# A vision-transformer tower on one core: a ring of twelve exponentials, softmax sums turned in blocks on DVE, and V in two buffers

## What is computed

```python
qkv = fake_quant(x, sx1, zx1) @ fake_quant(ww1, sw1, zw1).T
q, k, v = jnp.split(qkv, 3, axis=-1)
dots = jnp.einsum('bhnd,bhmd->bhnm', fake_quant(q, sq, zq), fake_quant(k, sk, zk)) * scale
a = jax.nn.softmax(dots, axis=-1)
out = jnp.einsum('bhnm,bhmd->bhnd', fake_quant(a, sa, za), fake_quant(v, sv, zv))
return fake_quant(out, sx2, zx2) @ fake_quant(ww2, sw2, zw2).T + bb2
```

## Time and profile before

| what | value |
|---|---|
| median of 3 runs | 1808.92 us (1805.69 to 1816.67) |
| the profiled execution | 1809.49 us, its span 1807.5 us |
| busy: PE, DVE, ACT, POOL | 1448.1 (80%), 1430.0 (79%), 1023.6 (57%), 420.5 us (23%) |
| mean granted TensorE clock | 0.765 |
| chain that ended last | PE 51%, issue 19%, DVE 18%, ACT 7% |
| products pi, 384 | 380.7 us busy on DVE |
| reciprocals of the sums, 192 | 267.7 us busy on DVE |
| exponentials, 384 | 316.2 us busy on ACT, 255.1 us idle ahead of them |

### The profile page before, as it was taken

The page is one execution under the profiler, slowest core; times in us unless marked ns, Lnnn a source line. Parts: engine busy times, 40 slices in busy tenths (PEclk is TensorE's granted clock), DMA queues, the critical chain, the costliest instruction groups (busy, mean ns, idle before and its releaser), DMA issues.

```text
span 1807.5 us, 41731 instructions
## 1 busy us (share of the span) xinstructions
PE 1448.1 (80%) x11806; PEld 846.6 (47%) x11806; DVE 1430.0 (79%) x2863; ACT 1023.6 (57%) x2005; POOL 420.5 (23%) x540
## 2 busy tenths in 40 slices
PE   5999858888887878987898888888798476666765
PEld 5999824444444444444444444444444233333332
DVE  4557827878778787788878888777878789999997
ACT  0000035666666565566656666555656378888887
POOL 6444400000000000000000000000000166666664
PEclk9999956768769686589758787666957567778778
DMA  7899712222223232233223232222323222223232
GB/s 238 272 278 299 223 48 76 89 89 86 81 89 96 85 96 84 80 97 92 85 79 94 83 97 86 85 85 86 90 78 90 83 62 83 83 78 87 83 87 65
DMA packets 154934, 192.00 MB, mean 106 GB/s; under 512 B 40208, under 2 KB 117072, under 8 KB 154576
## 3 DMA queue, kind: packets, MB, share of 16 engines
q1 hardware_dynamic: 99120, 154.10, 28.4%
q10 hardware_dynamic: 55776, 37.45, 7.0%
HBM read 156.99 MB, written 34.50 MB: 106 GB/s over the span
## 4 chain that ended last, share of the span: by engine, by line
PE 51%; issue 19%; DVE 18%; ACT 7%; ACTq 2%; DMA 2%; DVEq 1%; POOL 0%; SPq 0%
PE psum L1054 10%; PE psum L1170 10%; PE psum L1110 8%; DVE pi L923 7%; PE psum L1158 5%; PE psum L1117 5%; PE psum L1127 4%; PE psum L1192 3%; PE psum L1129 2%; DVE qkb L787 2%; DVE xring L1012 2%; ACT qki L519 2%; ACT wraw L557 1%; DVE yb L1037 1%; ACT att L533 1%
## 5 line engine op out<-in xcount | busy, mean ns | idle before, releaser
L557 ACT ACTIVATE wraw<-psum 128x788 f32<-128x788 f32 (+1 forms) x384 | 316.2, 824 | 255.1 <-DVE pi L923 249.2
L902 DVE RECIPROCAL weff<-psum 128x197 f32<-128x197 f32 x192 | 267.7, 1394 | 213.8 <-PE psum L1170 213.8
L923 DVE TENSOR_TENSOR pi<-wraw,weff 128x788 int16<-128x788 f32 (+1 forms) x384 | 380.7, 991 | 0.3 <-DMA weff<-z_row 0.3
L701 POOL TENSOR_TENSOR h<-hin,att 128x192 f32<-128x192 f32 (+1 forms) x128 | 83.8, 655 | 1122.2 <-ACT att L533 1122.2
L1170 PE MATMUL psum<-wraw,sa_cols 128*32 128x197 f32 (+1 forms) x3072 | 270.2, 433 | 15.6 <-DVE weff L902 15.2
L1110 PE MATMUL psum<-xT,w1b 96*128 96x197 bf16 x1536 | 239.8, 310 | 43.2 <-ACT xT L515 43.2
L519 ACT ACTIVATE qki<-psum 128x394 int16<-128x394 f32 x384 | 178.3, 494 | 89.1 <-PE psum L1110 88.3
L1110 PEld LDWEIGHTS psum<-xT,w1b 96*128 96x128 bf16 x1536 | 154.2, 118 | 148.9 <-issue 91.0
L1054 PE MATMUL psum<-weff,xring 128*128 128x192 f32 (+1 forms) x1168 | 196.7, 331 | 19.5 <-DVE weff L746 16.8
L787 DVE TENSOR_SCALAR pT<-pi,lo,hi 128x788 bf16<-128x788 int16 (+1 forms) x384 | 190.7, 497 | 24.9
L1054 PEld LDWEIGHTS psum<-weff,xring 128*128 128x128 f32 (+1 forms) x1168 | 192.8, 192 | 20.5 <-DVE weff L746 16.8
(11 more groups left out here) (108 smaller groups left out, 2017.1 us busy)
## 6 DMA issues: line engine op xcount, KB each, us to landing
weff<-z_row SPq DMA_DIRECT2D x192, 394.0 KB, 3.4
xring<-xt SPq DMA_DIRECT2D x98, 384.0 KB, 4.3
tin<-h_att SPq DMA_DIRECT2D x49, 192.0 KB, 2.5
tres<-h_att ACTq DMA_DIRECT2D x49, 192.0 KB, 2.6
out<-oo ACTq DMA_DIRECT2D x49, 192.0 KB, 2.6
h_res<-hp ACTq DMA_DIRECT2D x96, 96.0 KB, 3.8
hin<-h_res SPq DMA_DIRECT2D x64, 96.0 KB
h_att<-h SPq DMA_DIRECT2D x64, 96.0 KB
```

The source lines that it names most:

```text
L557: act.activation(ex[0:r, u, :, :].rearrange("p (a h) n -> p a h n", a=2), psum[0:r, 2 * (u % 2):2 * (u % 2) + 2, 0:2 * N] .rearrange("p a ...
L902: v.reciprocal(zinv[:, g, :], psum[:, 4, 0:N]).then_inc(s_zinv, 1)
L923: v.tensor_tensor(pi[0:r, t, :, 0:N], ex[0:r, w % U1, :, :], zb[0:r, g, :, :], ALU.mult).then_inc(s_pi, 1)
```

## The change

The arrays `wraw`, `weff`, `wmix` and `xring` become parts of one array `big`, so that `ex` can take twelve units instead of six. ACT's exponential now waits for the product twelve units back. The lags on DVE grow by two slots: TT_LAG 5 to 7, CLIP_LAG 6 to 8, and the pieces `o` of SLOTS move accordingly. V has two buffers ahead of its clip, and the clip moves from slot 1 to slot 5. The reciprocal of 128x197 becomes three operations: a turn of the sums out of PSUM in blocks of 32x32 (224 = 7 x 32 columns, the last 27 padded with ones), after which the 32 equal rows of a head are 32 equal columns; a reciprocal of one column of each of the seven blocks; a turn back into `zinv`. PE may overwrite the sums once they are turned.

```diff
-        wraw = sb("wraw", [128, KC, 5, D], fp32)
-        weff = sb("weff", [128, 4, KC, D], fp32)
-        wmix = sb("wmix", [128, 2, 2, D], fp32)
-        xring = sb("xring", [128, PACK, KC * 128], fp32)
+        NR, NF, ND = KC * 5 * D, 4 * KC * D, 4 * D
+        big = sb("big", [128, NR + NF + ND + PACK * KC * 128], fp32)
...
-        ex = stage[:, 0:24 * N].rearrange("p (u h n) -> p u h n", u=6, h=4)
+        NEX, NZ = 48 * N, 224
+        ex = big[:, 0:NEX].rearrange("p (u h n) -> p u h n", u=12, h=4)
+        zb = big[:, NEX:NEX + 12 * N].rearrange("p (g h n) -> p g h n", g=3, h=4)
+        zt = sb("zt", [128, NZ // 32, 32], fp32)
+        zti = sb("zti", [128, NZ // 32, 32], fp32)
+        zinv = sb("zinv", [128, 3, NZ], fp32)
...
-        SLOTS = [[("v", 3, 0), ("o", 2, -2), ("xt", 0, 1)],
+        SLOTS = [[("v", 3, 0), ("o", 1, -2), ("xt", 0, 1)],
                  [("qk", 0, 1), ("qk", 1, 1), ("v", 0, 1)],
-                 [("o", 0, -1), ("qk", 2, 1)],
+                 [("o", 2, -2), ("qk", 2, 1)],
                  [("qk", 3, 1), ("qk", 4, 1), ("qk", 5, 1)],
-                 [("o", 1, -1), ("y", 0, -2)],
+                 [("o", 0, -1), ("y", 0, -2)],
                  [("y", 1, -2), ("v", 1, 1), ("v", 2, 1)]]
...
-        TT_LAG, CLIP_LAG = 5, 6
+        TT_LAG, CLIP_LAG = 7, 8
...
-                        wait(act, s_vb, im)
+                        wait(act, s_vb, im - 1)
...
-                        wait(act, s_pi, U - 5)
+                        wait(act, s_pi, U - 11)
...
+                    summed = u % 2 == 0 and has_unit(b, u - 2)
+                    if summed:
+                        dve.wait_ge(s_zsum, G + 1)
+                        wait(dve, s_zti, G)
+                        v.transpose(zt[:, :, :].rearrange("p a b -> p (a b)"), psum[:, 4, 0:NZ]).then_inc(s_zt, 1)
                     if has_unit(b, u - CLIP_LAG):
...
-                    if u % 2 == 0 and has_unit(b, u - 2):
-                        G, g = 3 * b + u // 2 - 1, (u // 2 - 1) % 3
-                        dve.wait_ge(s_zsum, G + 1)
-                        v.reciprocal(zinv[:, g, :], psum[:, 4, 0:N]).then_inc(s_zinv, 1)
-                    if u == 1 and exists(b, 0):
+                    if summed:
+                        dve.wait_ge(s_zt, G + 1)
+                        wait(dve, s_zinv, G)
+                        v.reciprocal(zti[:, :, 0], zt[:, :, 0]).then_inc(s_zti, 1)
+                    if u == 5 and exists(b, 0):
...
+                    if summed:
+                        dve.wait_ge(s_zti, G + 1)
+                        wait(dve, s_zrow[g], 16 * (b - 1 if u == 0 else b))
+                        v.transpose(zinv[:, g, :], zti[:, :, :].rearrange("p a b -> p (a b)")).then_inc(s_zinv, 1)
...
-                            wait(pe, s_zinv, G)
+                            wait(pe, s_zt, G)
```

More of the change, by code:

```diff
@@ L90, in vit_tower_kernel @@
         xb = sb("xb", [128, 2, PACK, D], bf16)
-        stage = wraw[:, :, :, :].rearrange("p a b c -> p (a b c)")
+        stage = big[:, 0:NR]
         stage_i = sb("stage_i", [128, 2 * 3 * INNER], i16)
@@ L158, in vit_tower_kernel @@
         s_zsum = sem("softmax_summed")
+        s_pad = sem("softmax_sum_padded")
+        s_zt = sem("softmax_sum_turned")
+        s_zti = sem("softmax_inverse_step")
         s_zinv = sem("softmax_inverse_ready")
@@ L410, in spread @@
                     wait_apart(sp, s_zb[g], 16 * image)
-                    sp.dma_start(z_row[g, :, :], zinv[0:128:32, g, :]).then_inc(s_zrow[g], 16)
+                    sp.dma_start(z_row[g, :, :], zinv[0:128:32, g, 0:N]).then_inc(s_zrow[g], 16)
                     wait_apart(sp, s_zrow[g], 16 * image + 16)
@@ L526, in read_piece @@
                     if k == 0:
-                        wait(act, s_vb, im)
-                    act.activation(vi[0:r, t, half * W:(half + 1) * W], psum[0:r, bank, 0:W], ACT.Copy,
+                        wait(act, s_vb, im - 1)
+                    act.activation(vi[0:r, par if d == 0 else 1 - par, t, half * W:(half + 1) * W], psum[0:r, bank, 0:W], ACT.Copy,
                                    scale=factor[F_V]).then_inc(evac[kind], 1)
@@ L884, in _ @@
             ins.then_inc(s_mv, 1)
+            v.memset(psum[:, 4, N:NZ], 1.0).then_inc(s_pad, 1)
             quantise(LAST, 0, LAST, 2, 3, B)
@@ L1086, in _ @@
             pe.wait_ge(s_wq, 4)
+            pe.wait_ge(s_pad, 1)
             def product(b, par, n):
```

27 lines of the change are left out of this document (15 added, 12 removed).

## The result

| | before | after |
|---|---|---|
| median of 4 runs each, same chip | 1810.01 us (1805.69 to 1816.67) | 1545.24 us (1538.83 to 1546.87) |
| ratio, 95% interval | | 0.8528 [0.8491, 0.8565] |
| the profiled execution, its span | 1809.49, 1807.5 us | 1546.79, 1544.7 us |
| mean granted clock, whole run | 0.765 | 0.888 |
| busy: PE, DVE, ACT | 1448.1 (80%), 1430.0 (79%), 1023.6 (57%) | 1227.4 (79%), 1318.9 (85%), 994.9 (64%) |

The change saves 265 us, 15%. The forecast was 1634 with a range down to 1550: the measured time lies 5 us under the range, 9 us under the second rival (1554).

A forecast was written before the change was run, and what follows sets the result against it. DVE was taken to bound attention at full clock, PE at half clock. At 13.8 and 20.7 us an image and clock 0.85, 15.33 instead of 18.21 us over 61 images saves 176: 1634 us, range 1550 to 1740.

The forecast's parts named there:

- the second rival: Attention loop: the clock hardly falls any more (half clock 5%), 14.03 us an image, -255 us, 1554 us; chance 0.15.
- the choice of the mean clock: Attention loop: mean clock 0.85, half clock 30% of the time instead of 50%, chosen between 0.75 and 1.00.
- Two levels, and which engine bounds at which: Attention images: DVE sets the pace at full clock, 13.8 us after the change; PE at half clock, 20.7 us.
- DVE's work, 13.7 us: DVE per image: 10.96 us without reciprocals plus three groups of 0.90 us, bounds 12.9 and 15.25 us.
- lost in phase: Full-clock image: 0.1 us that DVE and PE lose to each other, added to DVE's 13.7 us, giving 13.8.
- The ring: Twelve exponentials: ScalarE is freed, PE's 1.2 and 0.7 us waits go; PE's idle time collects before the scores, some 1.2 us.
- The lags: DVE's products run seven slots behind instead of five, told as part of what frees ScalarE; no size of their own.
- V: V's clip moves from slot 1 to slot 5, its reads no longer wait; same work, nothing gained or lost.
- The spread of the inverse: SP's store and second load of the inverse: 6.1 us with the product, needed after 11.5 us, so hidden.
- The first: Rival, attention loop: the clock's share stays 0.75, 16.56 us an image, -101 us, 1709 us; chance 0.15.
- the fifth: Rival: PE's remaining idle time, at one place each image, holds the clock down; all half clock, +152, 1961 us; chance 0.04.
- The third and fourth: Rivals, turns dear: only PE's waits shift, 1759 us, chance 0.08; or no measurable change, 1800 us, chance 0.03.

The follow-up runs named there:

- ring_only: The kernel after with the one old reciprocal in place of the three operations; 1740.75 us, ratio 0.9692 to the kernel before.
- dve_11: The kernel after with an unused DVE product of 128x950 floats in slot 5, behind the clip of k; 1627.02 us, ratio 0.9059 to the kernel before.
- dve_11_s4: The kernel after with the same unused 128x950 DVE product in slot 4, ahead of the clip of k; 1900.42 us, ratio 1.0577 to the kernel before.
- turns_only: The kernel after with a ring of six, the old lags and one V buffer, keeping the three operations; 1792.1 us, ratio 0.9912 to the kernel before.
- fill_before: The kernel before with unread matmuls, three ahead of an "o" piece and four ahead of the scores of slot 5; 1740.28 us, ratio 0.9689.
- dve_05_s4: The kernel after with an unused DVE product of 128x400 floats in slot 4, ahead of the clip of k; 1606.49 us, ratio 0.8924 to the kernel before.
- v_one: The kernel after with one buffer for V and its clip back in slot 1; 1579.9 us, ratio 0.8793 to the kernel before.
- lag5: The kernel after with DVE's lags and the place of the "o" pieces as before; 1543.94 us, ratio 0.8576 to the kernel before.
- k_first: The kernel after with k clipped at the head of DVE's slot 4, ahead of the turn; 1600.12 us, ratio 0.8899 to the kernel before.
- k_xq: k_first with SP's load of xq issued ahead of the spread of group 2; 1544.26 us, ratio 0.858 to the kernel before.
- lag5_k: lag5 with the clip of k at the head of slot 4, as in k_first; 1573.84 us, ratio 0.8751 to the kernel before.
- ring_fill: ring_only with seven unread matmuls of 384 columns in PE's gap at the scores; 1594.39 us, ratio 0.8873 to the kernel before.

## Why the prediction was wrong, point by point

**The step that failed is the choice of the mean clock.** It put half clock at 30% of the time (0.85); the rows of the loop after show 1.00 over 720 us, and the clock from 300 to 1125 us is 0.99. The working of the prediction with 13.8 us for each image gives 61 x (15.33 - 13.8) = 93 us less than it said, 1541 us; 1546.8 were measured in the profiled execution. The third and fourth distance between reads of xT, at half clock, are 5.3 and 4.6 us over 13.8. These 9.9 us are more than the 6 that are left, so the rest of the working is off by some 4 us the other way.

Why was 0.85 chosen? The working took PE's mean busy share, 74% and 86%, and chose a clock between no change and the best. The share alone doesn't tell it: in a full-clock image of ring_only PE is busy 78% of the time and in one of dve_11 79%, and the clocks are 0.76 and 0.93. (A clock that doesn't follow PE's busy share was one of the prediction's own signs of being wrong.) Here are the kernels with PE's idle time in one image at full clock (the image less PE's busy time, so up to 0.1 us off the sum of the waits), and what the clock did. For dve_11_s4 it is the sum of the waits from 924 to 940 us:

| kernel | image us | PE idle us | largest gap us | clock | falls |
|---|---|---|---|---|---|
| before | 15.9 | 4.1 | 1.1 | 0.75 | 31 |
| turns_only | 15.8 | 4.1 | 1.4 | 0.73 | 34 |
| ring_only | 15.0 | 3.3 | 1.9 | 0.76 | 26 |
| dve_11_s4 | | 3.3 | 2.1 | 0.59 | 12 |
| fill_before | 16.5 | 3.3 | 0.8 | 0.91 | 10 |
| dve_11 | 14.7 | 3.1 | 1.0 | 0.93 | 11 |
| dve_05_s4 | 14.2 | 2.7 | 1.6 | 0.93 | 6 |
| v_one | 14.4 | 2.7 | 1.1 | 1.00 | 0 |
| lag5 | 13.8 | 2.3 | 1.1 | 1.00 | 0 |
| after | 13.7 | 2.2 | 1.1 | 0.99 | 1 |
| k_first | 13.7 | 2.1 | 0.7 | 0.91 | 12 |
| k_xq | 13.7 | 2.1 | 0.7 | 0.97 | 4 |
| lag5_k | 13.6 | 2.0 | 0.7 | 0.90 | 12 |
| ring_fill | 14.7 | 2.0 | 0.8 | 0.99 | 0 |

The rows with 3.1 to 3.3 us of idle time run from 0.59 to 0.93: with a largest gap of 2.1 and 1.9 us the clock is 0.59 and 0.76, with one of 0.8 and 1.0 us it is 0.91 and 0.93. The two with 2.7 us differ the same way. But the largest gap alone doesn't tell it either: the kernel before has no gap over 1.2 us, as the prediction said, and sits at 0.75 with 4.1 us of waits near each other. So in these kernels both count, how much PE idles and how much of it lies in one place. It is not a rule, though: the three kernels with the clip of k moved have as little idle time as any, no gap over 0.7 us in the image taken, and 4 to 12 falls. In k_first single waits for xq reach 1.4 us; k_xq and lag5_k have no such wait, and what brings their clock down is open.

The kernel after keeps the 1.1 us gap at the scores, but of the others 1.2 us are left of 3.0. Taking for each of the 31 falls before the largest of PE's waits in the 6 us ahead of it, that is the scores 14 times, ScalarE's bank at the product with V 8 times, att 7 times and xT twice (how far one looks back shifts some between the scores and att: with 4 us they are 10 and 11). The ones for the bank and for att are the waits that the ring took away. The prediction listed both as leaving, and said that the falls begin behind such waits; it didn't go on to count at which of them each fall begins, which the trace of before would have told.

The Trainium skill (TensorE: Matmul & The Clock Gate, A second HAM failure mode: psum-queue depth-cycling) describes a kernel in which short idle times between groups of matmuls make the clock go back and forth. The trace agrees: 31 falls with no gap over 1.2 us. It is nearer to this case than the long gaps of the section that the prediction cited.

**Two levels, and which engine bounds at which: right for the kernel after, half right for the one before.** At full clock DVE was named; an image takes 13.7 us and DVE has 12.89 of it, 94% (over 95% was forecast). But before, a DVE with less to do made an image hardly shorter (turns_only, 15.8 us), while the ring without it did (ring_only, 15.05 us). At half clock PE: 11.00 of 11.00 us in the dip. 20.7 us was forecast for an image there; the kernel after has none behind its start, but an image of turns_only at half clock takes 20.8 with 20.0 us of PE, a wait of 0.67 for xT and one of 0.2 for att.

**DVE's work, 13.7 us: 0.6 too much, and its wait 0.5 too little.** From start to next start, the operations of the image from 697.5 us come to 13.1 us: the turns and small reciprocals 2.58, that is 0.86 a group (0.90 forecast), the six products 5.95 (6.12 before), the six clips of pT 2.29 where they had 2.65, the other clips 2.3 where they had 2.2. So of the 0.6 us, 0.4 lie in operations that the prediction carried over unchanged from before, and 0.1 in the turns. The turn at 0.41 and the reciprocal at 0.19 lie 0.03 and 0.00 from the estimates from the earlier trace rows; the prediction's other estimate of a turn, 411 ns, is what was measured, and the sum of the three durations is the 1.01 us that went with it. That the period came out at 13.7 and not at 14.0 is due to starts that follow closer than the durations say, and to the smaller rest. The Trainium skill's rule to keep the number of operations down (VectorE: DVE Perf Modes, Rules for kernel authors) was cited against this edit: one operation of 1.39 us became three with 1.01 in sum, and the trace decides for it, since 7 columns are inverted instead of 197. DVE's wait for PE's sums, 0.54 us ahead of this image and 0.62 ahead of the next, takes the place of the 0.1 "lost in phase". The two errors nearly cancel, so that the 13.8 came out better than its parts, by luck.

**The ring: right.** ScalarE's wait for pi goes, with it PE's 1.2 and 0.7 us, and the wait for the first turn also. The place and size of the gap that PE keeps were forecast ("in front of the scores, some 1.2 us a time"): 1.1 is measured. Ring and turns also show why neither could be costed alone: with the ring of six DVE's gain vanishes in the ring (turns_only), with the old reciprocal most of what the ring could give is lost in the clock (ring_only, 64 us).

**The lags: nothing gained, right** (lag5), though the text told them as part of what frees ScalarE. **V: nothing gained, wrong**: 0.7 us an image, some 35 us (v_one). The step looked at the work and not at the waits: V's clip in slot 1 stands ahead of all of DVE's queue, and waits there for PE to finish with the old V. In the image of before that clip has no wait:

```profile
786.47 0.67 DVE L787 TENSOR_SCALAR vb<-vi,lo,hi 128x1536 bf16<-128x1536 int16 x1
```

So it is a wait that the faster loop brings. Since the sum counted only DVE's work, the error did not touch it.

**The spread of the inverse: hidden, right.** DVE's only wait in the image is the 0.54 us for the sums, and from 300 to 1125 us it waited for nothing else either (61 times, 42.5 us); none for the load of the inverse is there.

**The rivals.** The second (the clock hardly falls, 1554) is what happened, and had 0.15. Its reason, that the stretches ahead of the falls are full of waits that go, was the better one. The first (clock unchanged) is what befell ring_only (0.76), the fifth what befell dve_11_s4 (0.59): about 1 us more of DVE's work ahead of the clip of k is all that lies between the kernel after and a kernel slower than before. The third and fourth, which needed dear turns, are ruled out by the 409 and 407 ns of a turn.

## What to carry to other kernels

Cost a change at each level of the clock apart, then look where each fall of the clock begins and whether the change empties or deepens just that gap: at nearly the same sum of idle time (3.1 and 3.3 us) it mattered most how it lay, and a microsecond of DVE's work ahead of PE's largest gap cost four times what it did elsewhere. When two parts feed each other in a circle (a ring of buffers and the engine that frees it), neither alone shows its worth; time them together before dropping one. Where the clock is low and PE waits in one place, matmuls that nothing reads are a cheap test of whether the clock is the bound, and here were a gain of 65 and 146 us.
